# Linear attention: scaling the next batch's queries and keys ahead of this batch's spread inverses

## The reference

```python
def l2norm(x):
    return x * jax.lax.rsqrt(jnp.sum(x * x, -1, keepdims=True))

def _step(S, xs):
    qt, kt, vt, gt, bt = xs
    S = S * jnp.exp(gt)[..., None, None]
    pred = jnp.einsum('bhk,bhkv->bhv', kt, S)
    delta = (vt - pred) * bt[..., None]
    S = S + jnp.einsum('bhk,bhv->bhkv', kt, delta)
    return (S, jnp.einsum('bhk,bhkv->bhv', qt, S))

q = short_conv(hidden_states @ Wq, conv_wq).reshape(b, t, NUM_HEADS, HEAD_K)   # k and v in the same way
q = l2norm(q) * dk ** (-0.5)
k = l2norm(k)
o = o * jax.lax.rsqrt(jnp.mean(o * o, -1, keepdims=True) + EPS) * norm_weight
o = o * jax.nn.silu(gate)
```

## Time and profile before

| | |
|---|---|
| median of three runs | 1408.55 us (1402.6 to 1410.22) |
| the profiled execution | 1410.85 us, its span 1409.3 us |
| mean granted clock of TensorE | 0.93 |
| TensorE matmul busy | 1222.8 us (87% of the span) |
| TensorE weight load busy | 1040.2 us (74%) |
| VectorE busy | 939.5 us (67%) |
| ScalarE busy | 558.9 us (40%) |
| GpSimd busy | 112.6 us (8%) |

### The profile page before, as it was taken

One profiled execution on the slowest core, in us unless ns is written; L12 is line 12 of the kernel. 1 busy time (PEld: TensorE's weight loads), 2 busy tenths in 40 slices (PEclk: granted clock), 3 DMA queues, 4 the chain that ended last, 5 costly groups with the idle time before them and its releaser, 6 DMA issues. The chain is left out here.

```text
span 1409.3 us, 24031 instructions
## 1 busy us (share of the span) xinstructions
PE 1222.8 (87%) x8826; PEld 1040.2 (74%) x8826; DVE 939.5 (67%) x2715; ACT 558.9 (40%) x1394; POOL 112.6 (8%) x123
## 2 busy tenths in 40 slices
PE   4999999899999967999899985768989899898478
PEld 3888788788888856888788874557777677677255
DVE  3767467375555766565566675888889889885423
ACT  4634445353353543333343422334344335334211
POOL 1000000000000010000000010122022212202000
PEclk9999999999999967999999986788999999899689
DMA  8010000000000020000000010000000000000222
GB/s 272 1 61 1 1 1 1 0 0 0 0 1 0 1 83 0 1 1 1 3 1 1 1 46 28 25 26 2 27 27 26 2 27 26 2 2 1 90 71 102
DMA packets 25719, 33.94 MB, mean 24 GB/s; under 512 B 4780, under 2 KB 21004, under 8 KB 25612
## 3 DMA queue, kind: packets, MB, share of 16 engines
q1 hardware_dynamic: 25612, 32.52, 7.1%
HBM read 30.34 MB, written 2.17 MB: 23 GB/s over the span
## 5 line engine op out<-in xcount | busy, mean ns | idle before, releaser
L986 PE MATMUL b_ps<-ln_high,b_high 128*128 128x512 f32 x256 | 102.2, 399 | 26.7 <-PEq L61 20.9
L333 DVE TENSOR_REDUCE a_negmax<-a_ps 128x1 f32<-128x128 f32 x128 | 37.3, 291 | 115.2 <-PE a_ps L514 106.6
L889 DVE TENSOR_TENSOR gate_up_raw<-gate_up_raw,b_ps 128x512 f32<-128x512 f32 x64 | 43.3, 686 | 92.0 <-PE b_ps L986 60.0
L986 PE MATMUL b_ps<-ln_low,b_high 128*128 128x512 f32 x256 | 101.7, 397 | 0.0
L986 PE MATMUL b_ps<-ln_high,b_low 128*128 128x512 f32 x256 | 101.6, 397 | 0.0
L1013 PE MATMUL b_ps<-b_wd_high,b_mid 128*128 128x256 f32 x512 | 96.4, 283 | 0.0
L553 PE MATMUL a_ps<-a_wo_high,a_oT 128*128 128x256 f32 x512 | 94.5, 283 | 1.9 <-DVE a_oT L359 1.9
L945 ACT ACTIVATE gate_up_raw<-b_ps 128x512 f32<-128x512 f32 x64 | 37.5, 599 | 121.3 <-PE b_ps L986 121.2
L477 PE MATMUL a_ps<-ln_high,a_w_high 128*128 128x512 f32 x160 | 68.9, 430 | 15.1 <-PEq L61 15.1
L553 PEld LDWEIGHTS a_ps<-a_wo_high,a_oT 128*128 128x128 f32 x512 | 79.5, 188 | 2.8 <-DVE a_oT L359 2.8
L1013 PEld LDWEIGHTS b_ps<-b_wd_high,b_mid 128*128 128x128 f32 x512 | 80.6, 188 | 0.6
(11 more groups left out here) (356 smaller groups left out, 3181.0 us busy)
## 6 DMA issues: line engine op xcount, KB each, us to landing
d_slots<-in_D_packed SPq DMA_DIRECT2D x16, 433.0 KB, 4.5
c_a_all<-a_scratch SPq DMA_DIRECT2D x8, 768.0 KB, 3.6
x<-in_hidden SPq DMA_DIRECT2D x4, 512.0 KB, 10.9
a_raw<-in_A_q SPq DMA_DIRECT2D x4, 512.0 KB, 8.2
gate_up_raw<-in_A_o SPq DMA_DIRECT2D x1, 2048.0 KB, 13.8
gate_up_raw<-in_B_g SPq DMA_DIRECT2D x1, 2048.0 KB, 12.1
gate_up_raw<-in_B_u SPq DMA_DIRECT2D x1, 2048.0 KB, 8.6
b_wd<-in_B_d SPq DMA_DIRECT2D x1, 2048.0 KB, 9.2
```

Source lines behind the costliest of these rows:

```text
L333: nc.vector.tensor_reduce(negmax[:, h % 2, 2 * b:2 * b + 1], ps[:, SC[b], 0:P], AX_X, ALU.max, negate=True)
L889: nc.vector.tensor_tensor(product[:, m, :], silu[:, m, :], ps[:, UP[m], :], ALU.mult).then_inc(product_ready, 1)
L986: mm = nc.tensor.matmul(ps[:, bank, :], wpart, xpart, start=(j == 0), stop=(j == len(passes) - 1))
```

## The change

GpSimd scales the queries of batch 0 ahead of the loop, and in each turn those of batch t + 1, behind the squares and ahead of this batch's spread inverses; before, the turn began with those of batch t. VectorE scales the keys of batch 0 ahead of the loop, and in each turn those of batch c = t + 1 behind the last column sum, ahead of the last step of the convolution, the first spread inverse and epsilon. The instructions, their shapes and their waits are the same.

```diff
@@ -1690,11 +1690,12 @@
                     for p in range(1, PAIRS):
                         spread_inverse(nc.gpsimd, p, "td_pool")
 
+                queries(0)
                 for t in range(BATCH + 2):
-                    run(t, queries)
                     run(t - 2, gated_outputs)
                     run(t, decayed_keys)
                     run(t + 1, all_squares)
+                    run(t + 1, queries)
                     run(t, inverses)
 
             @block.vector
@@ -1839,11 +1840,13 @@
                     for q in range(first, to):
                         channels.conv(dve, c, q)
 
+                def keys(m):
+                    for part in KEYS_AT:
+                        normalise_channels(dve, nc.vector, m, part, "kq_vector")
+
+                keys(0)
                 for t in range(BATCH + 2):
                     c, m, s, d = t + 1, t, t - 1, t - 2
-                    for part in KEYS_AT:
-                        if inside(m):
-                            normalise_channels(dve, nc.vector, m, part, "kq_vector")
                     run(m, scan, 0)
                     run(m, scan, 1)
                     if s == LAST:
@@ -1931,6 +1934,7 @@
                     run(m, column_product, 15)
                     run(s, mean_square, 1)
                     run(m, column_sum, 15)
+                    run(c, keys)
                     run(c, convolve, 17, 18)
                     run(m, first_inverse)
                     run(s, add_epsilon)
```

## The result

The changed kernel takes 1413.34 us (median of 20 runs, 1407.83 to 1415.65) against 1408.62 us of the kernel before (20 runs, 1402.32 to 1411.62): ratio 1.003, 95% interval 1.0018 to 1.0041. It is 4.7 us slower, clear of noise, and the forecast was 1413.2. With 20 runs of each kernel a difference smaller than the 7 us that the prediction named can be told from no change: the interval is 2.5 to 5.8 us. The profiled execution took 1413.85 us with a span of 1412.3, 3.0 us more than the profile of before.

The account below looks back on a forecast made before the run. Bounds at batch boundaries: TensorE's 2.54 us wait for queries, VectorE and GpSimd holding each other up, ScalarE between epsilon and TensorE. Boundary terms 5.8 + 0.35 + 1.15 - 2.7 gave +4.6 us: 1413.2 us, range 1401 to 1420.5.

Parts of the forecast that it names:

- Queries beside the column products: GpSimd scaling queries before the spread inverses may hold up VectorE's column products: 0.3 us taken, bounds 0 and 0.6.
- Keys behind the last column sum: VectorE's keys take 1.6 us beside GpSimd's spread; scores start 1.9 us after the last column sum, 2.5 us earlier.
- Epsilon behind the gating multiply: VectorE's epsilon waits for GpSimd's 1.81 us multiply, ending 4.9 us after the last column sum, 2.25 us later.
- The second way: GpSimd goes ahead of VectorE's spread, which ends 5.0 us after the last column sum, epsilon just after: the same outcome.
- Gate and first inverse product: ScalarE's 2.3 us chain frees the PSUM bank late, so TensorE's first inverse product starts 2.0 us later.
- VectorE gains nothing: VectorE reaches the first products 1 us earlier (bounds 0 and 2.3), then waits for ScalarE's later taps.
- The 24 matmuls: TensorE's inverse products keep taking 4.4 us, so the second scores start 1.45 us later (ends 0.6 and 2.4).
- first rival: Behind TensorE's longer idle time the clock stays low, products take 5.3 us at six boundaries: 1419.2 us, chance 0.22.
- C, the low clock: Rival theory tested in the experiments: the low clock behind TensorE's longer idle time is the loss; no chance given.
- the delay is kept: From the second scores to the next batch's last column sum nothing changes, so the 1.45 us delay stays.
- Epsilon early: Rival: VectorE's epsilon gets in before GpSimd's gating multiply, the PSUM bank frees as now, about -4 us: 1404.6 us, chance 0.16.
- as drawn: Rival: VectorE and GpSimd contention falls away, VectorE gains 1 us at six boundaries, -8.7 us: 1399.9 us, chance 0.17.

Follow-up runs that it names:

- scans early only: Changed kernel with the next batch's first two scans made in the turn before, epsilon left where the change puts it: 1414.6 us, ratio 1.0033.
- the last pair: Kernel before and changed kernel, each with epsilon directly behind the last column sum and the first two scans a turn earlier: 1403.95 and 1383.57 us.
- both limits moved: Changed kernel with epsilon directly behind the last column sum and the next batch's first two scans made in the turn before: 1383.37 us, ratio 0.981.

## Why the prediction was right, and where its parts were not

The total, 1413.2 against 1413.34, is closer than its terms. By the prediction's steps:

1. *Queries beside the column products*, taken at 0.3 us: 0.2 us. Right.
2. *Keys behind the last column sum*, taken at 1.6 us with the scores at T+1.9: 1.62 us and T+1.7. Right.
3. *Epsilon behind the gating multiply*, T+4.9: T+4.7. Right, and shown by two runs that put another GpSimd instruction there (0.69 us behind a short one, 1.77 behind the long one). The second way that the step allowed, in which GpSimd goes ahead of VectorE's spread, did not happen.
4. *Gate and first inverse product*, T+7.2, with the 0.3 us of step 1 T+7.5: T+7.0 and T+7.14. The 0.3 us has no place in these distances: it lies ahead of T, and delays T itself. In the sum over a batch it counts the same.
5. *VectorE gains nothing*. Its gain was larger than the bound I gave: the first products begin at T+5.8 instead of T+8.5, 2.7 us against a bound of 2.3, because the first scan fell into the 0.6 us in which GpSimd waits for the root, and the second was not held either (0.66 us; GpSimd's next multiply took 1.87 us beside it). The 2.40 us wait for the taps ate it, as said, and the run with the scans early only shows that more of it would not help.
6. *The 24 matmuls*, taken at 4.4 us: 5.2 to 5.5 us at boundaries 3 to 6, because the clock stayed low for 6.8 us. That was the first rival's price (5.3), so its mechanism came true at boundaries 3 to 6. The second scores start at T+12.3 to T+12.5 there, 1.9 us late in the mean, between the 1.45 of the forecast and the 2.4 of the rival; so C, the low clock, is a part of the loss and not its start. At the second boundary they were 0.04 us late (forecast 0.35), at the seventh 1.39 (forecast 1.15). At the first they were 3.2 us early (forecast 2.7). Together that is +5.8 us at the second scores, against +4.6 in the sum.

The sentence that failed is the one behind step 6, that the delay is kept from there on. From T to V the changed kernel loses 5.3 us; from V to T it got 3.0 us back, although the queries cost 0.2 us a batch there, because of the clock behind the second idle time. In the profiled pair this leaves 2.3 us, and 0.7 of the 3.0 us of span lie outside the boundaries; the medians are 4.7 apart. Each kernel's own runs spread over 8 to 9 us, and the spread goes with the clock: of the changed kernel's 20 runs, the nine of 1407.8 to 1412.7 us have a mean granted clock of 0.933 or 0.934, and the ten of 1413.4 to 1415.7 us 0.929 or 0.930. The kernel before, as measured beside the last pair, has four runs of 1402.4 to 1403.1 us at 0.939 to 0.941 and twelve of 1406.1 to 1411.0 us at 0.930 to 0.936. With one profile of each kernel I can't say in which batches the other runs had their low stretches, nor why a low stretch comes or not behind the same idle time. So the terms are shown at one execution, and that the total agrees to 0.1 us is luck: the forecast stands for a loss of 4.6 us that is kept, and the profiled pair shows a larger one of which more than half is given back.

Epsilon early (-4 us) did not come about in the change, and "as drawn" neither. In that last rival I called 8.7 us the most that VectorE's queue allows. For this change nothing contradicts it, but the run with both limits moved shows 25 us to be had once the scans leave the tail. I had looked at VectorE's queue as fixed.

## What to carry to other kernels

Before a late operand is moved forward, list every wait of the instruction behind it with its time: here the next one, a PSUM bank released through a 12-element operation, a root and a table load, had 0.6 us of slack against 2.5 us of expected gain. An instruction is also moved in front of things on other engines: taking 1.8 us of short multiplies out of GpSimd's queue drew a long one forward onto VectorE's most urgent small operation. And an edit that measures slower may be worth keeping on trial: this one cost 4.7 us alone and brought 20.4 us beside two others.

## What the runs showed of the hardware

Some of VectorE's instructions wait until a GpSimd instruction is over, whatever their own size: the same 12 elements took 0.16 us alone, 0.69 us behind the last 0.6 us of a short multiply, 1.03 us beside a spread, 1.77 us beside the gating multiply. It can be more than one, and there the prediction's "until that instruction is over" is too short. In the kernel before, the first scan asks during GpSimd's second query multiply, which ends at 1075.42, lets the gating multiply go ahead as well and ends at 1077.75:

```profile
1074.87 2.88 DVE L1705 TENSOR_TENSOR_SCAN cb_E<-c_a_all,c_ident 128x256 f32<-128x256 f32 x1
```

Others weren't held: convolution steps, which read one of their two tensors from PSUM, took 0.46 to 0.49 us beside GpSimd, and the column sum beside the moved queries took 0.33 us, against 0.32 without them. The Trainium skill says in "GPSIMD Engine Reference", section "Key points", that GpSimd shares its SBUF interfaces with VectorE and contends with instructions in a two-port mode or with two SBUF inputs. The scans and the convolution steps agree with it, and the scans go against the narrower note that the prediction weighed (two-input scans take 4.11 or 1.26 us a pair by what GpSimd does beside them). Epsilon has one tensor as input; whether it runs in a two-port mode no trace shows.

I had not expected the clock to pay back. At the fourth boundary an idle time of 2.27 us was followed by 3.4 us at 1.2 GHz in one kernel and an equal one of 2.26 us by none in the other. In the kernel before, such a stretch is worth 1.2 to 1.6 us a batch (V to T of 24.2 to 24.6 against 22.98 us). It doesn't take a change in the kernel: in the version with both limits moved, boundaries 2 to 6 are alike, 22.47 or 22.48 us from T to V and 2.26 or 2.27 us of idle time, and boundaries 3, 5 and 6 have the low stretch behind it while 2 and 4 do not. Differences of some 3 us between versions of this kernel can come from that alone.
